# Attention in plain float32: scores and V product without split operands, the mask added in PSUM, one maximum per group

## The chip, the core and the metric

The kernel runs on one core of a Trainium2 chip. The metric is the device time of one execution in microseconds. The core has five engines that work through their own instruction queues and wait for each other by semaphores: TensorE (PE in the profile; its weight loads are PEld), VectorE (DVE), ScalarE (ACT), GpSimd (POOL, called the Pool here) and SyncE (SP), which starts transfers here.

## The reference, cut to what matters

Eight batches of 256 rows with 256 columns go through a cross attention with 16 heads and then through a mixture of eight experts. Both have a layer norm ahead and a residual. The attention is the part that changes:

```python
kv_c = kv @ W_kvc
q_c = q @ W_dq
q_nope = (q_c @ W_uq).reshape(b, lq, H, HD).transpose(0, 2, 1, 3)
q_rope = (q_c @ W_qr).reshape(b, lq, H, R).transpose(0, 2, 1, 3)
...
scores = (jnp.einsum('bhqd,bkhd->bhqk', q_nope, k_nope) + jnp.einsum('bhqr,bkr->bhqk', q_rope, k_rope)) * scale
k_ids = jnp.arange(lk)[None, None, :]
qs = seg_id[:, :, None]
good = (k_ids <= qs) & (k_ids >= qs - LOOKBACK)
scores = jnp.where(good[:, None, :, :], scores, NEG)
attn = jax.nn.softmax(scores, axis=-1)
out = jnp.einsum('bhqk,bkhd->bqhd', attn, v).reshape(b, lq, H * HD)
return out @ W_o
```

The feed forward part computes all eight experts (`relu(x @ expert_w + expert_b)`, 256 to 256 each) and averages the two with the highest gate logits. All data are float32. A row sees at most nine keys, and the segment ids are such that all of them lie in the first 128 keys; a second path for other ids exists in the kernel and isn't taken.

## The kernel before

Weights are folded beforehand: W_uk into W_uq, W_uv into W_o, so that a head works on vectors of 128 (64 latent, 64 rotary) against keys `kT` and on values `v` of 64. Rows are worked in 16 tiles of 128. A group is four heads of one tile (`HG = 4`), so there are 64 groups, four per tile and eight per batch.

The work is a software pipeline written out by hand in `slot(b, k)`, one such function for each engine, called by `walk`. Slot i works on several groups at once. In the order of TensorE's queue it holds: the query product of group i+1 (three products of float32r parts, 512 columns), the scores of group i, the four transposes of prob of group i-1, the product with W_o of group i-2, the gate product in one slot of four, the four transposes of q of group i+1, the transposes of x2n in one slot of four, the experts of group i-8 (a bf16 product of three rows that adds the bias, then six of 512 columns) and the V product of group i-1. In the slots 1 to 7 the latent product `latent` (L504) and transposes of the next batch's rows (`x_turn`, L489) stand in the place of the experts. Slots of batches 2 to 6 run in a loop of eight slots (`Fori`), the others are written out.

Products for which float32 accuracy is wanted are made of float32r parts: an operand is split into a rounded `hi` and the rest `lo`, and `mm3` adds hi by hi, hi by lo and lo by hi. For the scores both operands are split: ScalarE casts the transposed q to `qT_hi` (L1011), VectorE subtracts to `qT_lo` (L1235), and `kT_hl` holds both parts of the keys side by side, split once a batch by VectorE (L1251, L1253). Per head one product of qT_hi with both halves (256 columns, L883) and one of qT_lo with the first half (128 columns, L884) fill one of four 256-column strips in two PSUM banks. VectorE then adds the mask to the second half of the strips (`s2m`, L1192), and for each head one step (L1199) adds the halves, scales by -SCALE, writes the negated scores `nsc` to SBUF and their minimum to `nmax`. ScalarE computes four exponentials from `nsc` (L1023) with their sums, VectorE the reciprocals (L1272), and the Pool scales prob (L1114). After the transposes ScalarE casts to `pT_hi` (L1007) and VectorE subtracts to `pT_lo` (L1218). The V product (mm3, L550 to L552) uses `v_hi` and `v_lo`, which hold the 64 columns of v between two blocks of zeros, so that a slice of 128 weight columns puts the even heads on the lower and the odd ones on the upper half of the partitions: six products of 256 columns, all with 128 weight columns.

The Pool builds the mask of the next tile in three steps over slots g = 1 to 3 (L1100, L1104, L1109). VectorE's two rope products (L1176, L1177) and the Pool's join (L1062) stand between the query product and the transposes of q (L924). At the start `fold_o` (L446) folds W_uv into W_o by plain float32 products with 64 weight columns; their output goes to the lower and the upper 64 partitions in turn.

Of the kernel before, what the change touches and what calls it, by code (L numbers as in the profile page):

```python
# [53 lines left out]
def kernel_program(nc, x, ctx_t, itok, w_kvc, w_dq, w_uq_t, w_qr, w_uk_t, w_kr, w_uv_t, w_o,  # L54
                   gate_w, gate_b, expert_w, expert_b, rope, w_kvc_t, out):
    with ExitStack() as ctx:
# [20 lines left out]
        ident = sb("ident", [P, P])  # L77
        kidx = sb("kidx", [P, P])
# [13 lines left out]
        v_hi, v_lo = sb("v_hi", [P, 3, KVC], F32R), sb("v_lo", [P, 3, KVC], F32R)  # L92
# [94 lines left out]
        def _(act):  # L187
# [56 lines left out]
        def _(dve):  # L244
# [22 lines left out]
            dve.tensor_copy(kidx[:], kidx_i[:]).then_inc(S("kidx_done"), 1)  # L267

# [96 lines left out]
        def gb(name, shape, dt=F32):  # L365
# [21 lines left out]
        qT_hi = [sb(f"qT_hi{i}", [P, HG, P], F32R) for i in range(2)]  # L387
        qT_lo = [sb(f"qT_lo{i}", [P, HG, P], F32R) for i in range(2)]
        nsc = [sb(f"nsc{i}", [P, HG, P]) for i in range(2)]
# [4 lines left out]
        pT_hi = [sb(f"pT_hi{i}", [P, HG, P], F32R) for i in range(2)]  # L394
        pT_lo = [sb(f"pT_lo{i}", [P, HG, P], F32R) for i in range(2)]
        oT_hi = [sb(f"oT_hi{i}", [P, 2, P], F32R) for i in range(2)]
        oT_lo = [sb(f"oT_lo{i}", [P, 2, P], F32R) for i in range(2)]
        kT_hl = sb("kT_hl", [P, 2, P], F32R)
        s2m = sb("s2m", [P, HG, P])
        m_after, m_before, mask = sb("m_after", [P, P]), sb("m_before", [P, P]), sb("mask", [P, P])  # L400
# [3 lines left out]
        B_S = psum[:, 4 * 512:6 * 512].rearrange("p (h a n) -> p h a n", h=HG, a=2)  # L404
# [11 lines left out]
                 "nope_copied", "qT_hi_done", "exp_done", "pT_hi_done", "oT_hi_done", "xT_hi_done", "relu_done",  # L416
                 "rope_parts", "qT_lo_done", "score_max", "recip_done", "pT_lo_done", "oT_lo_done", "x2_done",
                 "ln_step", "x2n_done", "xT_lo_done", "gates_ready", "gate_step", "logit_part", "qc_split", "mask_step", "k_split",
                 "v_split", "v_hi_done", "x_normed", "x_turned", "x_columns", "latent_mm", "latent_sb", "wo_hi_done",
                 "wo_lo_done", "fold_o_mm", "we_hi_done", "we_lo_done", "k_hi_done", "qc_hi_done", "s2_masked", "waits_passed",  # L420
# [9 lines left out]
        def live(i, end):  # L430
            return not isinstance(i, int) or 0 <= i < end
# [427 lines left out]
        def _(pe):  # L859
            def slot(b, k):  # L860
# [28 lines left out]
                if live(i - 1, GROUPS):  # L889

                    at_least(pe, "prob_normed", i)
                    at_least(pe, "pT_hi_done", i - 1)
                    at_least(pe, "pT_lo_done", i - 1)
# [23 lines left out]
                if live(i + 1, GROUPS):  # L917
# [3 lines left out]
                    at_least(pe, "qT_hi_done", i + 1)  # L921
                    at_least(pe, "qT_lo_done", i + 1)
# [36 lines left out]
                if live(i - 1, GROUPS):  # L959

                    if (k - 1) % SLOTS == 0:
                        at_least(pe, "v_split", b + (k - 1) // SLOTS + 1)
# [385 lines left out]
```

## Time and profile before

| | us |
|---|---|
| median of 3 runs | 456.32 (456.17 to 457.66) |
| span of the profiled execution | 454.5 |

| engine | busy us | share of the span |
|---|---|---|
| TensorE, products | 422.4 | 93% |
| TensorE, weight loads | 355.9 | 78% |
| VectorE | 365.4 | 80% |
| ScalarE | 289.3 | 64% |
| Pool | 265.7 | 58% |

The profiled execution's own time is known by its span, from its first to its last instruction; the median of the runs is 1.8 us more. Busy time says that an engine had an instruction under way. TensorE's instructions overlap: the records of a product and of the next one cover each other, so the share of TensorE is not the share of its peak. What a block of products costs is read from the times at which it and the block behind it start. The share is also a mean over stages: the preparation up to some 26 us, the early slots to 87 us, the even stretch of 54 slots to 417 us, and the drain, in which experts alone are left.

### The profile page before, as it was taken

To read this page: it belongs to the slowest core of one execution; us is meant where nothing else is said; L and a number is where in the kernel's file an instruction comes from. 1 tells how busy PE (TensorE), PEld (TensorE's weight loads), DVE (VectorE), ACT (ScalarE), POOL (GpSimd) and SP (SyncE) were. 2 spreads that over 40 slices of the span, in tenths; PEclk is the share of its full clock that TensorE was granted. 3 is DMA by queue.
4 is the path that set the end of the run, shared out by engine and by line. 5 is a ranking of instruction groups with operands and counts; after the bars stand their busy time and mean duration, and the time that the engine had idled before them with its cause. 6 is when DMAs were issued, how large, how long until landed. Compare 5 with 4: busy or idle time off the path is not lost.

```text
span 454.5 us, 10511 instructions
## 1 busy us (share of the span) xinstructions
PE 422.4 (93%) x2702; PEld 355.9 (78%) x2702; DVE 365.4 (80%) x1369; ACT 289.3 (64%) x940; POOL 265.7 (58%) x365
## 2 busy tenths in 40 slices
PE   2966998899999999999999999999999999999995
PEld 2835887778888888878888888788888888788763
DVE  2659989897888888888889798988888888978541
ACT  1224766667676767677766767676776677667632
POOL 4033646647666747575765657575746575664545
PEclk9967999999999999999999999999999999999999
DMA  9990000000000000000000000000000000000000
GB/s 216 276 377 18 2 1 1 0 3 1 12 2 13 1 14 2 12 0 12 0 0 12 0 12 0 12 0 12 0 12 0 12 0 12 2 2 12 2 12 29
DMA packets 16530, 12.54 MB, mean 28 GB/s; under 512 B 7568, under 2 KB 16128, under 8 KB 16240
## 3 DMA queue, kind: packets, MB, share of 16 engines
q1 hardware_dynamic: 13488, 10.64, 7.9%
q10 hardware_dynamic: 2880, 1.43, 1.4%
q8 instruction: 14, 0.23, 0.2%
q14 instruction: 20, 0.16, 0.1%
q0 software_dynamic: 128, 0.09, 0.1%
HBM read 10.04 MB, written 2.10 MB: 27 GB/s over the span
## 4 chain that ended last, share of the span: by engine, by line
issue 39%; PE 25%; POOL 19%; DVE 7%; ACT 2%; POOLq 1%; DVEq 0%; ACTq 0%
POOL acc L1088 7%; PE psum L550 6%; PE psum L552 5%; PE psum L551 5%; POOL acc L1091 3%; PE psum L924 2%; PE psum L883 2%; PE psum L895 2%; POOL m_after L1100 2%; POOL m_before L1104 2%; POOL q_sb L1062 2%; ACT prob L1023 1%; DVE xn L477 1%; PE psum L954 1%; POOL rstd L1074 1%
## 5 line engine op out<-in xcount | busy, mean ns | idle before, releaser
L1114 POOL TENSOR_TENSOR prob<-prob,prec 128x512 f32<-128x512 f32 x64 | 68.6, 1071 | 91.6 <-DVE prec L1272 91.6
L1023 ACT ACTIVATE prob<-nsc,nmax 128x128 f32<-128x128 f32 x256 | 99.8, 395 | 3.7 <-DVE nmax L1199 3.7
L1062 POOL TENSOR_TENSOR q_sb<-rope_a,rope_b 128x256 f32<-128x256 f32 x64 | 47.0, 735 | 56.2 <-DVE rope_b L1177 56.2
L1199 DVE CUSTOM_DVE_ANT_0 nsc<-psum,s2m 128x128 f32<-128x128 f32 x256 | 59.1, 287 | 13.8 <-DVE s2m L1192 13.8
L1044 ACT ACTIVATE eout<-psum,gates 128x256 f32<-128x256 f32 x128 | 54.0, 477 | 19.0 <-DVE gates L1281 9.5
L1011 ACT CAST qT_hi<-psum 128x512 fp32r<-128x512 f32 x64 | 37.6, 587 | 43.7 <-PE psum L924 43.6
L883 PE MATMUL psum<-kT_hl,qT_hi 128*128 128x256 f32 x256 | 63.1, 324 | 0.0
L884 PE MATMUL psum<-kT_hl,qT_lo 128*128 128x128 f32 x256 | 57.4, 224 | 0.0
L550 PE MATMUL psum<-we_hi,xT_hi 128*128 128x512 f32 x128 | 57.2, 447 | 0.0
L884 PEld LDWEIGHTS psum<-kT_hl,qT_lo 128*128 128x128 f32 x256 | 49.6, 194 | 2.7
L883 PEld LDWEIGHTS psum<-kT_hl,qT_hi 128*128 128x128 f32 x256 | 48.9, 191 | 2.7
L552 PE MATMUL psum<-we_hi,xT_lo 128*128 128x512 f32 x128 | 50.5, 394 | 0.0
L551 PE MATMUL psum<-we_lo,xT_hi 128*128 128x512 f32 x128 | 50.3, 393 | 0.0
L1091 POOL TENSOR_TENSOR acc<-acc,eout 128x256 f32<-128x256 f32 x64 | 46.7, 729 | 5.0
L1023 ACT ACTIVATION_READ_ACCUMULATOR prob<-nsc,nmax 128x1 f32 x256 | 49.0, 191 | 0.0
L1192 DVE TENSOR_TENSOR s2m<-psum,mask 128x512 f32<-128x512 f32 x64 | 43.9, 686 | 3.9 <-PE psum L884 0.8
L999 ACT COPY q_sb<-psum 128x256 f32<-128x256 f32 x64 | 23.9, 373 | 36.3 <-DVE rope_b L1177 35.6
L924 PE MATMUL psum<-ident,q_sb 128*128 128x128 f32 x256 | 41.0, 284 | 5.6 <-POOL q_sb L1062 4.5
L1166 DVE TENSOR_TENSOR oT_lo<-psum,oT_hi 128x256 fp32r<-128x256 f32 x64 | 26.9, 420 | 21.3 <-ACT oT_hi L1029 21.2
L1218 DVE TENSOR_TENSOR pT_lo<-psum,pT_hi 128x512 fp32r<-128x512 f32 x64 | 43.9, 686 | 0.0
L1235 DVE TENSOR_TENSOR qT_lo<-psum,qT_hi 128x512 fp32r<-128x512 f32 x64 | 43.4, 677 | 0.3 <-ACT qT_hi L1011 0.3
L1029 ACT CAST oT_hi<-psum 128x256 fp32r<-128x256 f32 x64 | 23.8, 371 | 29.5 <-PE psum L552 29.4
(145 smaller groups left out, 1153.0 us busy)
## 6 DMA issues: line engine op xcount, KB each, us to landing
wo_raw<-in_w_o SPq DMA_DIRECT2D x2, 1024.0 KB, 10.6
we_raw<-in_expert_w SPq DMA_DIRECT2D x1, 2048.0 KB, 14.7
out<-acc SPq DMA_DIRECT2D x16, 128.0 KB, 1.7
x_all<-in_x SPq DMA_DIRECT2D x2, 640.0 KB, 7.8
ctxT<-in_ctx_t SPq DMA_DIRECT2D x2, 512.0 KB, 7.3
wuqT<-in_w_uq_t ACTq DMA_DIRECT2D x1, 768.0 KB, 13.1
wukT<-in_w_uk_t SPq DMA_DIRECT2D x1, 512.0 KB, 11.1
x_all<-in_x SPq DMA_DIRECT2D x1, 512.0 KB, 12.9
```

The lines of the kernel that those rows point to most:

```text
L550: pe.matmul(out_ap, l_hi, r_hi, start=start, stop=False)
L551: pe.matmul(out_ap, l_hi, r_lo, start=False, stop=False)
L552: return pe.matmul(out_ap, l_lo, r_hi, start=False, stop=stop)
L883: pe.matmul(B_S[:, h, :, :], qT_hi[r][:, h, :], kT_hl[:], start=True, stop=False)
L884: mm = pe.matmul(B_S[:, h, 0, :], qT_lo[r][:, h, :], kT_hl[:, 0, :], start=False, stop=True)
L924: mm = pe.transpose(B_QT[:, P * h:P * h + P], q_sb[1 - r][:, h, :], ident[:])
L1023: e = act.activation(prob[r][:, h, :], nsc[r][:, h, :], ACT.Exp, bias=nmax[r][:, h:h + 1], scale=-1.0, accum_out=psum_h[r][:, h:h + 1])
L1044: a = act.activation(eout[r][:, e, :], expert_bank(f)[:, O * e:O * e + O], ACT.Relu, scale=gates[j][:, 2 * kc + e:2 * kc + e + 1])
L1062: pool.tensor_tensor(q_sb[1 - r][:, :, KVC:P], rope_a[1 - r][:], rope_b[1 - r][:], ALU.add).then_inc(m["rope_joined"], 1)
L1091: pool.tensor_tensor(acc[j][:], acc[j][:], eout[1 - r][:, 1, :], ALU.add).then_inc(m["acc_step"], 1)
L1114: pool.tensor_tensor(p[:], p[:], prec[r][:, :].unsqueeze(2).to_broadcast([P, HG, P]), ALU.mult).then_inc(m["prob_normed"], 1)
L1199: e = dve.tensor_tensor_reduce(nsc[r][:, h, :], B_S[:, h, 0, :], s2m[:, h, :], -SCALE, BIG, ALU.add, ALU.min, nmax[r][:, h:h + 1])
```

## The change

The scores are one plain float32 product per head (`qT` as it comes out of the transposes, keys from `kT_all`), and the V product is two plain float32 products with 64 weight columns (`v_cur`), written to the lower and the upper half of the partitions. The casts to `hi` on ScalarE become copies of the same size; the subtractions `qT_lo`, `pT_lo`, the splits of k and v and the tiles for them are gone. `kT_all` is scaled by SCALE when it is copied in the preparation. The mask is held in bf16, in two buffers, and a product of a bf16 identity with the mask (512 columns, the mask repeated for four heads) starts each group's bank, to which the heads' scores are added. The scores of a group fill one bank, and two banks alternate. VectorE takes one maximum over the bank for all four heads, and ScalarE's exponentials read PSUM. Waits change with this: the scores wait for the exponentials of two groups before instead of the maximum of the last, and, in a tile's first group, for the mask.

```diff
@@ -210,8 +211,8 @@
-                act.copy(kT_all[:, 4 * i:4 * i + 4, :],
-                         bank[i].rearrange("p (b k) -> p b k", b=4)).then_inc(S("kT_sb"), 1)
+                act.mul(kT_all[:, 4 * i:4 * i + 4, :],
+                        bank[i].rearrange("p (b k) -> p b k", b=4), SCALE).then_inc(S("kT_sb"), 1)
...
@@ -224,9 +225,6 @@
-            pool.memset(v_hi[:].bitcast(F32), 0.0).then_inc(S("v_zero"), 1)
-            pool.memset(v_lo[:].bitcast(F32), 0.0).then_inc(S("v_zero"), 1)
...
@@ -265,6 +263,8 @@
+            dve.wait_ge(S("ident_done"), 1)
+            dve.tensor_copy(ident16[:], ident[:]).then_inc(S("ident16_done"), 1)
...
-        B_S = psum[:, 4 * 512:6 * 512].rearrange("p (h a n) -> p h a n", h=HG, a=2)
+        B_S = [bank[4 + i].rearrange("p (h n) -> p h n", h=HG) for i in range(2)]
...
@@ -874,14 +870,15 @@
-                    if k % SLOTS == 0:
-                        at_least(pe, "k_split", b + k // SLOTS + 1)
-                    at_least(pe, "qT_hi_done", i + 1)
-                    at_least(pe, "qT_lo_done", i + 1)
-                    at_least(pe, "score_max", i)
+                    at_least(pe, "qT_sb", i + 1)
+                    at_least(pe, "exp_done", i - 1)
+                    if g == 0:
+                        at_least(pe, "mask_step", 4 * (t + 1))
+                    keys = kT_all[:, bass.ds(b + k // SLOTS, 1), :].rearrange("p a n -> p (a n)")
+                    pe.matmul(B_S[r], ident16[:], mask[(k // GPT) % 2][:, :].unsqueeze(1).to_broadcast([P, HG, P]),
+                              start=True, stop=False)
                     for h in range(HG):
-                        pe.matmul(B_S[:, h, :, :], qT_hi[r][:, h, :], kT_hl[:], start=True, stop=False)
-                        mm = pe.matmul(B_S[:, h, 0, :], qT_lo[r][:, h, :], kT_hl[:, 0, :], start=False, stop=True)
+                        mm = pe.matmul(B_S[r][:, h, :], qT[r][:, h, :], keys, start=False, stop=(h == HG - 1))
...
@@ -969,14 +963,9 @@
                     q1 = 1 - r
-                    o = B_O[:, 0:D]
                     for odd in range(2):
-                        w = slice(KVC - KVC * odd, P + KVC - KVC * odd)
-                        vh = v_hi[:].rearrange("p a n -> p (a n)")[:, w]
-                        vl = v_lo[:].rearrange("p a n -> p (a n)")[:, w]
-
-                        mm = mm3(pe, o, vh, vl, pT_hi[q1][:, odd::2, :], pT_lo[q1][:, odd::2, :],
-                                 start=(odd == 0), stop=(odd == 1))
+                        mm = pe.matmul(B_O[KVC * odd:KVC * odd + KVC, 0:D], v_cur[:], pT[q1][:, odd::2, :],
+                                       start=True, stop=True)
...
@@ -1020,7 +1009,7 @@
-                        e = act.activation(prob[r][:, h, :], nsc[r][:, h, :], ACT.Exp, bias=nmax[r][:, h:h + 1], scale=-1.0,
+                        e = act.activation(prob[r][:, h, :], B_S[r][:, h, :], ACT.Exp, bias=nmax[r][:, h:h + 1],
...
@@ -1105,8 +1094,8 @@
-                    at_least(pool, "s2_masked", i + 1)
-                    pool.tensor_tensor(mask[:], m_before[:], m_after[:], ALU.add).then_inc(m["mask_step"], 1)
+                    at_least(pool, "s_done", i - 3)
+                    pool.tensor_tensor(mask[(k // GPT + 1) % 2][:], m_before[:], m_after[:], ALU.add).then_inc(m["mask_step"], 1)
...
@@ -1181,24 +1170,12 @@
-                    dve.tensor_copy(v_hi[:, 1:2, :], kv).then_inc(m["v_hi_done"], 1)
-                    dve.wait_ge(m["v_hi_done"], bv + 1)
-                    dve.tensor_tensor(v_lo[:, 1:2, :], kv, v_hi[:, 1:2, :].bitcast(F32), ALU.subtract).then_inc(m["v_split"], 1)
+                    dve.tensor_copy(v_cur[:], kv.rearrange("p a n -> p (a n)")).then_inc(m["v_ready"], 1)
                 if live(i, GROUPS):
 
                     at_least(dve, "s_done", i + 1)
-                    if g == 0:
-                        at_least(dve, "mask_step", 4 * (t + 1))
-                    dve.tensor_tensor(s2m[:], B_S[:, :, 1, :], mask[:, :].unsqueeze(1).to_broadcast([P, HG, P]),
-                                      ALU.add).then_inc(m["s2_masked"], 1)
-                if live(i, GROUPS):
-                    at_least(dve, "s2_masked", i + 1)
                     at_least(dve, "exp_done", i - 1)
-                    carry_wait()
-                    for h in range(HG):
-                        e = dve.tensor_tensor_reduce(nsc[r][:, h, :], B_S[:, h, 0, :], s2m[:, h, :], -SCALE, BIG,
-                                                     ALU.add, ALU.min, nmax[r][:, h:h + 1])
-                    e.then_inc(m["score_max"], 1)
+                    dve.tensor_reduce(nmax[r][:], B_S[r], AX.X, ALU.max, negate=True).then_inc(m["score_max"], 1)
...
@@ -1212,11 +1189,6 @@
-                if live(i - 1, GROUPS):
-                    at_least(dve, "pT_hi_done", i)
-                    at_least(dve, "pv_done", i - 2)
-                    dve.tensor_tensor(pT_lo[1 - r][:], B_PT[:, :].rearrange("p (h n) -> p h n", h=HG),
-                                      pT_hi[1 - r][:].bitcast(F32), ALU.subtract).then_inc(m["pT_lo_done"], 1)
...
@@ -1229,11 +1201,6 @@
-                if live(i + 1, GROUPS):
-                    at_least(dve, "qT_hi_done", i + 2)
-                    at_least(dve, "s_done", i)
-                    dve.tensor_tensor(qT_lo[1 - r][:], B_QT[:, :].rearrange("p (h n) -> p h n", h=HG), qT_hi[1 - r][:].bitcast(F32),
-                                      ALU.subtract).then_inc(m["qT_lo_done"], 1)
```

## Rows read from the trace of the kernel before

**Rows 1.** The page, part 1: busy us (share of the span) and instructions of TensorE and VectorE.

```profile
PE 422.4 (93%) x2702; PEld 355.9 (78%) x2702; DVE 365.4 (80%) x1369; ACT 289.3 (64%) x940; POOL 265.7 (58%) x365
```

**Rows 2.** Timeline of TensorE, one slot (start us, length us, engine, line, operation, tiles).

```profile
246.76 0.40 PE L550 MATMUL psum<-wq_hi,qc_hi 96*128 96x512 f32 x1
...
247.45 0.28 PE L883 MATMUL psum<-kT_hl,qT_hi 128*128 128x256 f32 x1
...
248.33 0.62 PE L895 MATMUL psum<-ident,prob 128*128 128x128 f32 x4
...
249.49 0.60 PE L924 MATMUL psum<-ident,q_sb 128*128 128x128 f32 x4
250.03 0.38 PE L954 MATMUL psum<-bias,ones 3*128 3x512 bf16 x1
...
251.60 0.39 PE L552 MATMUL psum<-we_hi,xT_lo 128*128 128x512 f32 x1
251.83 0.28 PE L550 MATMUL psum<-pT_hi,v_hi 128*128 128x256 f32 x1
...
252.54 0.40 PE L550 MATMUL psum<-wq_hi,qc_hi 96*128 96x512 f32 x1
```

**Rows 3.** Waits of weight loads, 87.4 to 417 us (waiter, releaser, total us, times, longest).

```profile
PEld psum L924 <- POOL q_sb L1062: 4.0, 14, 0.3
```

**Rows 4.** Busy time by stretch (length; PE, PEld, DVE, ACT, POOL; granted clock, DMA).

```profile
87.40:417.00 329.60, 325.94 (x2132) 278.48 (x2133) 283.93 (x1082) 230.75 (x767) 206.47 (x280) 1.00 0.02 6
...
48.87:87.32 38.45, 34.32 (x234) 29.37 (x233) 35.34 (x120) 26.62 (x89) 22.33 (x25) 1.00 0.01 1
```

**Rows 5.** Chain that ended last, in order of time, 20 to 90 us (start, length).

```profile
33.54 0.69 DVE qT_lo L1235
...
34.69 1.65 DVE st_all L155 x5
...
38.31 0.61 DVE s2m L1192
...
40.05 1.21 DVE wo_lo L456 x2
...
58.77 0.67 PE psum L924 x4
...
65.02 0.67 PE psum L924 x4
...
87.32 0.47 PE psum L550
```

**Rows 6.** Timeline of TensorE: plain float32 products, latent and in the preparation.

```profile
53.00 1.03 PE L504 MATMUL psum<-xnT,wdq 128*96 128x256 f32 x4
...
16.49 0.39 PE L333 MATMUL psum<-wcat,ctxT 128*128 128x128 f32 x2
```

**Rows 7.** Line L504 alone (length ns: shortest, median, longest; first and last start).

```profile
L504 PE MATMUL psum<-xnT,wdq x28: 379/379/379, 46.7 to 85.1; 128*96 128x256 f32 x28
```

**Rows 8.** Timeline of the weight loads in the slot of rows 2: the bias.

```profile
250.02 0.09 PEld L954 LDWEIGHTS psum<-bias,ones 3*128 3x128 bf16 x1 [0.17 <-issue]
```

**Rows 9.** Timeline of TensorE, 32.4 to 35 us: folding of W_o and its neighbours.

```profile
32.46 0.42 PE L924 MATMUL psum<-ident,q_sb 128*128 128x128 f32 x1
32.81 1.99 PE L446 MATMUL psum<-wo_raw,wuvT 128*64 128x256 f32 x16
34.73 0.50 PE L550 MATMUL psum<-wq_hi,qc_hi 96*128 96x512 f32 x1
```

**Rows 10.** Instructions by line and shape (count; busy us, mean ns; idle before).

```profile
L1192 DVE TENSOR_TENSOR s2m<-psum,mask 128x512 f32<-128x512 f32 x64 | 43.9, 686 | 3.9 <-PE psum L884 0.8
L1218 DVE TENSOR_TENSOR pT_lo<-psum,pT_hi 128x512 fp32r<-128x512 f32 x64 | 43.9, 686 | 0.0
...
L1261 DVE CAST qc_hi<-qc_all 96x128 fp32r x10 | 3.3, 335 | 0.0
...
L1261 DVE CAST qc_hi<-qc_all 96x128 fp32r<-96x128 f32 x6 | 1.6, 267 | 1.9 <-issue 1.9
```

More of the change, by code:

```diff
@@ L77, in kernel_program @@
         ident = sb("ident", [P, P])
+        ident16 = sb("ident16", [P, P], BF16)
         kidx = sb("kidx", [P, P])
@@ L89, in kernel_program @@
         flag = sb("flag", [1, 1], I32)
-        v_hi, v_lo = sb("v_hi", [P, 3, KVC], F32R), sb("v_lo", [P, 3, KVC], F32R)
+        v_cur = sb("v_cur", [P, KVC])
         block_sems = {}
@@ L386, in kernel_program @@
         rope_b = [sb(f"rope_b{i}", [P, HG, R]) for i in range(2)]
-        qT_hi = [sb(f"qT_hi{i}", [P, HG, P], F32R) for i in range(2)]
-        qT_lo = [sb(f"qT_lo{i}", [P, HG, P], F32R) for i in range(2)]
-        nsc = [sb(f"nsc{i}", [P, HG, P]) for i in range(2)]
+        qT = [sb(f"qT{i}", [P, HG, P]) for i in range(2)]
         nmax = [sb(f"nmax{i}", [P, HG]) for i in range(2)]
@@ L393, in kernel_program @@
         prec = [sb(f"prec{i}", [P, HG]) for i in range(2)]
-        pT_hi = [sb(f"pT_hi{i}", [P, HG, P], F32R) for i in range(2)]
-        pT_lo = [sb(f"pT_lo{i}", [P, HG, P], F32R) for i in range(2)]
+        pT = [sb(f"pT{i}", [P, HG, P]) for i in range(2)]
         oT_hi = [sb(f"oT_hi{i}", [P, 2, P], F32R) for i in range(2)]
         oT_lo = [sb(f"oT_lo{i}", [P, 2, P], F32R) for i in range(2)]
-        kT_hl = sb("kT_hl", [P, 2, P], F32R)
-        s2m = sb("s2m", [P, HG, P])
-        m_after, m_before, mask = sb("m_after", [P, P]), sb("m_before", [P, P]), sb("mask", [P, P])
+        m_after, m_before = sb("m_after", [P, P]), sb("m_before", [P, P])
+        mask = [sb(f"mask{i}", [P, P], BF16) for i in range(2)]
         B_Q, B_E, B_QT, B_PT, _, _, B_Y, B_X = bank
-        B_S = psum[:, 4 * 512:6 * 512].rearrange("p (h a n) -> p h a n", h=HG, a=2)
+        B_S = [bank[4 + i].rearrange("p (h n) -> p h n", h=HG) for i in range(2)]
         B_O = B_X
@@ L415, in kernel_program @@
         names = general_names + ["q_done", "qT_done", "s_done", "pT_done", "pv_done", "y_done", "xT_done", "gate_done", "e_done",
[L416 to L420, printed above, removed]
+                 "nope_copied", "qT_sb", "exp_done", "pT_sb", "oT_hi_done", "xT_hi_done", "relu_done",
+                 "rope_parts", "score_max", "recip_done", "oT_lo_done", "x2_done",
+                 "ln_step", "x2n_done", "xT_lo_done", "gates_ready", "gate_step", "logit_part", "qc_split", "mask_step",
+                 "v_ready", "x_normed", "x_turned", "x_columns", "latent_mm", "latent_sb", "wo_hi_done",
+                 "wo_lo_done", "fold_o_mm", "we_hi_done", "we_lo_done", "qc_hi_done", "waits_passed",
                  "rope_joined", "prob_normed", "rstd2_done", "acc_step", "out_stored0", "out_stored1"]
@@ L961, in slot @@
                     if (k - 1) % SLOTS == 0:
[L962 to L964 removed]
+                        at_least(pe, "v_ready", b + (k - 1) // SLOTS + 1)
+                    at_least(pe, "pT_sb", i)
                     at_least(pe, "oT_hi_done", i - 1)
@@ L1006, in slot @@
                     at_least(act, "pv_done", i - 2)
-                    act.copy(pT_hi[1 - r][:], B_PT[:, :].rearrange("p (h n) -> p h n", h=HG)).then_inc(m["pT_hi_done"], 1)
+                    act.copy(pT[1 - r][:], B_PT[:, :].rearrange("p (h n) -> p h n", h=HG)).then_inc(m["pT_sb"], 1)
                 if live(i + 1, GROUPS):
@@ L1010, in slot @@
                     at_least(act, "s_done", i)
-                    act.copy(qT_hi[1 - r][:], B_QT[:, :].rearrange("p (h n) -> p h n", h=HG)).then_inc(m["qT_hi_done"], 1)
+                    act.copy(qT[1 - r][:], B_QT[:, :].rearrange("p (h n) -> p h n", h=HG)).then_inc(m["qT_sb"], 1)
                 if g == 3 and live(t - 1, TILES):
@@ L1245, in slot @@
                     top_two("gate_step", t - 2, [3, 4])
-                bk = b + (k + 1) // SLOTS
-                if (k + 1) % SLOTS == 0 and live(bk, B):
-                    at_least(dve, "s_done", SLOTS * bk)
-                    kk = kT_all[:, bass.ds(bk, 1), :].rearrange("p a n -> p (a n)")
-                    dve.tensor_copy(kT_hl[:, 0, :], kk).then_inc(m["k_hi_done"], 1)
-                    dve.wait_ge(m["k_hi_done"], bk + 1)
-                    dve.tensor_tensor(kT_hl[:, 1, :], kk, kT_hl[:, 0, :].bitcast(F32), ALU.subtract).then_inc(m["k_split"], 1)
                 tq = TPB * b + k // GPT + 1
```

8 lines of the change are left out of this document (2 added, 6 removed).

## The prediction

> **What bounds the kernel now.** I read the busy shares first, then TensorE's order of work in one slot of the steady stretch, then who waits for whom. TensorE is busy 93% of the span, VectorE 80% [rows 1]. A busy TensorE proves little, since its instructions overlap: the pitch from start to start has to tell. In the slot that starts at 246.76 every block follows the last one without a gap [rows 2]: three query products to 247.45 (0.69 us), scores to 248.33 (0.88), transposes of prob and the output product to 249.49 (1.16), transposes of q to 250.03 (0.54), experts to 251.83 (1.80), V product to 252.54 (0.71): 5.78 in all. From 87.4 us on the clock is granted in full [rows 4], and the only data for which TensorE's loads wait are 14 late q_sb, 4.0 us in all [rows 3]; none waits for prob, pT or the scores. There the order of TensorE sets the time, and all that VectorE saves is worth those waits. Before 87.32 it is otherwise: six slots take 38.45 us [rows 4], and the chain runs from the transposes of q over exponentials, VectorE's xn, rope and the Pool's join back to the transposes, from 58.77 to 65.02, 6.25 long [rows 5]. VectorE's large subtractions aren't in that loop.
>
> **TensorE's blocks after the change.**
>
> Scores. Each of the four heads had one product of 256 columns and one of 128, with 0.22 a head [rows 2]. By the pace of the 512-column query products (0.23 each) their 384 columns would stream in 0.17: it is the two weight loads that fill the head's time. A plain float32 product appears as two records with a weight load each: the latent product is two products in the code and four records in the trace, which at 256 columns and full clock lie (1.03 - 0.38) / 3 = 0.22 apart, twice their columns' time [rows 6, 7]. With 128 columns the same form stands in the preparation: two records in 0.39 [rows 6], and a record alone lasts about 0.38 - 0.11 = 0.27 (128 columns less), so they are 0.11 to 0.12 apart. Eight of them make 0.90, so +0.02; ends 0 and +0.08. Streaming costs more, but the loads cost as much already. The Trainium skill (FP8 and Floating Point Precision, TensorE Precision Notes) says that true FP32 takes four passes through the array. The latent product's rows agree, but by columns alone the scores would go from 384 to 512 a head and cost a third more (+0.29), and by the row of the preparation they don't.
>
> Mask. One more product of 512 columns, in bf16 with 128 x 128 weights, goes ahead of the scores. Nearest row: a 512-column product among its like, 0.23 [rows 2]. The only bf16 product in the trace, the experts' bias with three rows, costs more. Its load starts at 250.02, 0.07 before the transposes end (249.49 + 0.60), and stood 0.17 idle [rows 2, 8]; the experts' block of 1.80 is six products at 0.23 (1.39) and 0.41 more. So the bias costs up to 0.58. Ends: 0.21 (the columns alone) and 0.58. But the plain float32 product with 64 weight columns shows the same hold of a load until the product ahead has nearly ended (below), while the products with 96 rows or columns show none: few rows or columns go with the hold, not bf16. The mask's uses all 128 by 128, so I take 0.23.
>
> V product. Six f32r products at 0.12 (0.71) become two plain float32 ones with 64 weight columns, four records. The folding of W_o has the same form: 128 x 64 weights, 256 columns, the two halves of the partitions in turn. Its 16 records at full clock take 1.99, so they are (1.99 - 0.38) / 15 = 0.107 apart, half of the latent product's pitch: two run side by side. They start at 32.81, 0.07 before the product ahead ends (32.46 + 0.42), and the query product behind starts at 34.73 and lasts 0.50 instead of 0.40 [rows 9, 2]. From 32.81 to 34.73 are 1.92 us; eight pairs at 0.215 are 1.72, so the edges cost 0.20 beyond them, and two pairs would take 0.43 + 0.20 = 0.63. In the slot the experts' last product ends at 251.60 + 0.39 = 251.99, so V's first load starts at 251.92 and the query product at 252.55: where it starts now. Only the query block grows by the exposed load, 0.10. So +0.11 for both. Ends: no hold at either side, 0.43 for 0.71 (-0.28); no records side by side, two more pitches (+0.54). I take +0.11, since [rows 9] show its very form. The rule that stands behind them is in the Trainium skill (TensorEngine Tiling, Key Properties): changing the tiling mode drains TensorE. It speaks against this edit, which leaves 128 weight columns for 64 and goes back once a slot; the rows agree.
>
> A slot grows by 0.02 + 0.23 + 0.11 = 0.36 us. The groups 8 to 63 have their scores and V products in the TensorE-bound part: 56 x 0.36 = +20.2 us.
>
> **What is given back.** VectorE loses s2m (0.69 us), four score steps (some 0.86), pT_lo (0.69) and qT_lo (as long), and gains one maximum over 128 x 512 in PSUM, which I price like s2m's one pass, 0.7 [rows 10]: 2.2 us less a slot. In the steady stretch this is worth the waits for q_sb, which stand behind rope and the Pool's join. The transposes of q now come 0.11 + 0.23 + 0.02 later in the slot, which covers a wait of 0.28: -4.0 [rows 3]. In the early slots the added 0.36 fits (5.78 + 0.36 is under 6.25), and six turns of 6.25 are 37.5 instead of 38.45: -1.0. At the start qT_lo and the split of kT (33.54 to 34.69) and s2m with the score steps (38.31 to 40.05) lie on the chain [rows 5]: 1.15 + 1.74 - 0.7 = 2.2 off; the first slots run in part at half clock and pay some 0.6 more for mask and scores: -1.6.
>
> At nothing I cost: the small copy to ident16 and the two fills that go (VectorE and the Pool wait for loads and TensorE then); the exponentials from PSUM instead of SBUF, as no wait of TensorE names prob, with 0 to 0.28 a slot if that cover went and the waits came back 56-fold; the bank pair, which replaces a wait for the maximum by one for exponentials two groups back. Keys and v_cur's source are addressed by a register: VectorE's qc_hi takes 335 ns so, and 267 with a fixed address [rows 10], so 0 to 0.07 for each of four products, 0.28 a slot. I take none, since TensorE's instructions queue ahead of their data.
>
> Sum: 454.5 + 20.2 - 4.0 - 1.0 - 1.6 = 468.1 us of span. The median of the runs stands 1.8 above the profiled span, so 469.9.
>
> **The rivals.**
> 1. As forecast, slower, 470: chance 0.71. Its own bounds: -0.1 a slot if a part of the hold is missed (-5.6), or +0.03 for the scores (+1.7) and q_sb waits that stay (+4.0): 464 to 476.
> 2. The mask's bf16 product holds the loads at both sides as the bias does, 0.35 more a slot, or the register addresses cost 0.28: 56 times, +16 to +20, 486 to 490. For: every bf16 product in the trace has the hold. Against: so have the float32 ones with few columns. Chance 0.15.
> 3. The V product goes without the hold: its loads slip in behind the experts' last product and the query product follows at once. A slot then changes by -0.28 + 0.23 + 0.02 = -0.03, and 456.3 - 1.7 - 6.6 = 448.0: faster. It decides once the V product with its edges takes under 0.58 (then 56 slots add just the 6.6 given back). For: the side-by-side pitch of 0.107 is real. Against: the hold is there in [rows 8, 9]. Chance 0.09, and 0.04 for an outcome near that point.
> 4. VectorE's 2.2 us a slot show in the steady stretch after all; then TensorE must have waited for it, and [rows 3] leave 4.0 us for that. Chance 0.01, faster.
>
> A measurement of this kernel can tell about 0.3% from no change. From these cases: faster 0.10, same 0.04, slower 0.86. The range leaves out the faster cases and the outer half of the second, and reaches down for a hold missed at one side: 462 to 487.
>
> **What would show it.** A mask product 0.23 before the first score; eight score records 0.11 to 0.12 apart; V's four records in 0.6, the first load 0.07 before the experts' end, and a query product of 0.50; slots without extras 6.14 long; no wait for q_sb after 90 us; VectorE near 50% of the span. The prediction is wrong if the mask's load waits for the end of the query product, if V's load overlaps the experts, or if the slots are longer than these blocks add up to.

## The result and the profile after

| | before | after |
|---|---|---|
| median of 6 runs, us | 456.25 (455.7 to 457.66) | 459.33 (458.34 to 460.19) |
| span of the profiled execution, us | 454.5 | 457.6 |

The ratio of the medians is 1.0061, with a 95% interval of 1.0044 to 1.0077: slower by 3.1 us, where 469.9 was forecast with a range of 462 to 487. The sign was right, and the size was missed by 10.6 us, below the range.

The busy shares of the page after, to be held against [rows 1]:

```profile
PE 431.5 (94%) x2638; PEld 317.1 (69%) x2638; DVE 250.6 (55%) x706; ACT 280.8 (61%) x940; POOL 264.9 (58%) x363
```

VectorE is busy for 115 us less, and TensorE for 9 us more. The time moved by 3, so the two don't simply exchange.

TensorE's timeline after, one slot without extras (start us, length us, engine, line, operation, tiles), to be held against [rows 2]:

```profile
264.28 0.50 PE L546 MATMUL psum<-wq_hi,qc_hi 96*128 96x512 f32 x1
...
265.09 0.39 PE L878 MATMUL psum<-mask,ident 128*128 128x512 bf16 x1
265.31 1.05 PE L881 MATMUL psum<-kT_all,qT 128*128 x8
266.21 0.60 PE L891 MATMUL psum<-ident,prob 128*128 128x128 f32 x4
266.56 0.37 PE L546 MATMUL psum<-wo_hi,oT_hi 128*128 128x256 f32 x1
...
267.36 0.60 PE L919 MATMUL psum<-ident,q_sb 128*128 128x128 f32 x4
267.89 0.38 PE L949 MATMUL psum<-bias,ones 3*128 3x512 bf16 x1
268.21 0.50 PE L546 MATMUL psum<-we_hi,xT_hi 128*128 128x512 f32 x1
...
269.80 0.65 PE L967 MATMUL psum<-pT,v_cur 128*64 128x256 f32 x4
270.38 0.50 PE L546 MATMUL psum<-wq_hi,qc_hi 96*128 96x512 f32 x1
```

From start to start: query product 0.81 us (0.69 in [rows 2]), mask 0.22, scores 0.90 (0.88), transposes and output product 1.15 (1.16), transposes of q 0.53 (0.54), experts 1.91 (1.80), V product 0.58 (0.71). That is 6.10 for 5.78. Records have an error of 0.01 each; over many slots the mask is 0.23, the scores 0.89, and the slots g = 0, 2 and 3, which wait in neither kernel, go from 6.22 to 6.51, from 5.79 to 6.09 and from 6.01 to 6.32: +0.30. The letter g is the place of a slot's group in its tile. A slot g = 1 goes from 6.03 to 6.10, or from 6.6 to 6.7 in seven cases, to 6.09.

The 54 slots from the start of slot 8 to that of slot 62, before and then after (stretch and length; PE, PEld, DVE, ACT, POOL; granted clock, DMA), and the waits of weight loads in this stretch after:

```profile
87.32:417.26 329.94, 326.28 (x2134) 278.82 (x2135) 284.26 (x1084) 230.83 (x767) 206.53 (x280) 1.00 0.02 6
82.67:420.46 337.79, 337.79 (x2083) 248.23 (x2081) 189.30 (x526) 224.55 (x770) 206.27 (x281) 1.00 0.02 6
```

```profile
PEld psum L546 <- issue: 33.4, 109, 0.4
PEld psum L967 <- issue: 19.1, 53, 0.4
PEld psum L878 <- issue: 14.7, 54, 0.3
PEld psum L949 <- issue: 9.1, 54, 0.2
PEld psum L967 <- DVE eq_in L1143: 0.4, 1, 0.4
```

Before, TensorE had no record under way for 329.94 - 326.28 = 3.66 us of it; after, it is busy in all of the 337.79. The late q_sb of [rows 3] are gone. So these 54 slots are 7.85 us longer, what lies ahead of them is 4.65 shorter (slot 8 starts at 82.67, not 87.32 as in [rows 5]), and the drain is the same to 0.1 us: +3.1.

But 54 x 0.30 is 16.2, not 7.85. Of the missing 8.35 us the waits of [rows 3] are 4.0. The rest is in the trace of before, where I had not seen it. The waits of TensorE's products before, 87.4 to 417 us (waiter, what ended the wait, total us, times, longest), then TensorE and VectorE around one of the seven:

```profile
PE psum L550 <- issue: 2.6, 7, 0.4
```

```profile
147.47 0.39 PE L552 MATMUL psum<-we_hi,xT_lo 128*128 128x512 f32 x1
148.22 0.36 PE L550 MATMUL psum<-pT_hi,v_hi 128*128 128x256 f32 x1 [0.37 <-issue]
...
149.01 0.40 PE L550 MATMUL psum<-wq_hi,qc_hi 96*128 96x512 f32 x1
```

```profile
144.56 0.76 DVE L1186 TENSOR_TENSOR v_lo<-kcat,v_hi 128x64 fp32r<-128x64 f32 x1
145.25 0.68 DVE L1192 TENSOR_TENSOR s2m<-psum,mask 128x512 f32<-128x512 f32 x1
...
147.34 0.68 DVE L1218 TENSOR_TENSOR pT_lo<-psum,pT_hi 128x512 fp32r<-128x512 f32 x1
```

In [rows 2] the V product starts 0.23 after the last expert product (251.60, 251.83); here 0.75 after it. It starts 0.20 after pT_lo ended (147.34 + 0.68 = 148.02), and its block is 0.79 long instead of 0.71. pT_lo is late because v_lo (0.76, once a batch) stands ahead of s2m, the score steps, x and pT_lo on VectorE. The seven come 48.8 to 48.9 us apart, once a batch: 7 x 0.60 = 4.2 us. 16.2 - 4.0 - 4.2 = 8.0, against 7.85 measured. After the change there is no pT_lo, and TensorE doesn't wait for one.

### The profile page after: what moved, and what is told of

Same layout as the page of the kernel before. It is cut to its first block, busy times and chain, and to the rows that moved or that the text cites. A ratio compares the mean times of both kernels' runs of the same rounds, so it can differ in the third digit from the quotient of the medians.

```text
span 457.6 us, 9458 instructions
## 1 busy us (share of the span) xinstructions
PE 431.5 (94%) x2638; PEld 317.1 (69%) x2638; DVE 250.6 (55%) x706; ACT 280.8 (61%) x940; POOL 264.9 (58%) x363
## 4 chain that ended last, share of the span: by engine, by line
PE 81%; POOL 4%; issue 3%; DVE 3%; ACT 2%; DVEq 0%; POOLq 0%; ACTq 0%
PE psum L546 17%; PE psum L548 12%; PE psum L547 12%; PE psum L881 11%; PE psum L967 7%; PE psum L919 6%; PE psum L891 5%; PE psum L949 4%; PE psum L878 3%; ACT prob L1012 1%; POOL q_sb L1051 1%; POOL acc L1077 1%; POOL acc L1080 1%; PE psum L442 1%; DVE xn L473 1%
## 5 line engine op out<-in xcount | busy, mean ns | idle before, releaser
L1012 ACT ACTIVATE prob<-psum,nmax 128x128 f32<-128x128 f32 x256 | 91.2, 377 | 0.0
L881 PEld LDWEIGHTS psum<-kT_all,qT 128*128 128x128 f32 x512 | 68.0, 193 | 1.6
L881 PE MATMUL psum<-kT_all,qT 128*128 (+1 forms) x512 | 67.5, 275 | 0.0
L1000 ACT COPY qT<-psum 128x512 f32<-128x512 f32 x64 | 37.5, 586 | 42.7 <-PE psum L919 42.7
L1012 ACT ACTIVATION_READ_ACCUMULATOR prob<-psum,nmax 128x1 f32 x256 | 55.2, 216 | 0.0
L1178 DVE TENSOR_REDUCE nmax<-psum 128x4 f32<-128x512 f32 x64 | 44.2, 690 | 16.0 <-PE psum L881 15.5
L996 ACT COPY pT<-psum 128x512 f32<-128x512 f32 x64 | 37.7, 588 | 19.2 <-PE psum L891 18.9
L546 PE MATMUL psum<-wo_hi,oT_hi 128*128 128x256 f32 x128 | 41.7, 326 | 1.0 <-DVE oT_lo L1155 1.0
L967 PE MATMUL psum<-pT,v_cur 128*64 128x256 f32 x256 | 41.7, 404 | 0.4 <-DVE xT_lo L1202 0.4
L891 PE MATMUL psum<-ident,prob 128*128 128x128 f32 x256 | 38.6, 273 | 1.3 <-POOL prob L1103 1.3
## 6 DMA issues: line engine op xcount, KB each, us to landing
wo_raw<-in_w_o SPq DMA_DIRECT2D x2, 1024.0 KB, 10.5
```

Source lines behind the costliest of these rows:

```text
L546: pe.matmul(out_ap, l_hi, r_hi, start=start, stop=False)
L881: mm = pe.matmul(B_S[r][:, h, :], qT[r][:, h, :], keys, start=False, stop=(h == HG - 1))
L891: mm = pe.transpose(B_PT[:, P * h:P * h + P], prob[1 - r][:, h, :], ident[:])
L967: mm = pe.matmul(B_O[KVC * odd:KVC * odd + KVC, 0:D], v_cur[:], pT[q1][:, odd::2, :], start=True, stop=True)
L1012: e = act.activation(prob[r][:, h, :], B_S[r][:, h, :], ACT.Exp, bias=nmax[r][:, h:h + 1], accum_out=psum_h[r][:, h:h + 1])
```

## The experiments

The theory: TensorE's order of work sets the time, an edit is worth its blocks, and the kernel before had two kinds of waits in the steady stretch (q_sb, pT_lo), which a longer slot covers. The rival: VectorE's load itself costs there, so that its relief is what was given back. Each expectation says what its own A and B stand for. All ratios are to the kernel before, with 95% intervals.

**The wait for pT_lo by itself.** The kernel before without v_lo:

```diff
-                    dve.tensor_copy(v_hi[:, 1:2, :], kv).then_inc(m["v_hi_done"], 1)
-                    dve.wait_ge(m["v_hi_done"], bv + 1)
-                    dve.tensor_tensor(v_lo[:, 1:2, :], kv, v_hi[:, 1:2, :].bitcast(F32), ALU.subtract).then_inc(m["v_split"], 1)
+                    dve.tensor_copy(v_hi[:, 1:2, :], kv).then_inc(m["v_split"], 1)
```

> The kernel before, with one thing left out: the low part of v is not computed (it stays zero, so the V product is computed from the high part of v alone). This takes one VectorE subtraction of 0.76 us out of the first V slot of each batch. Theory A: the seven slots of the kernel before in which the V product starts 0.5 us late (labelled issue) wait for VectorE's pT_lo, which stands behind this subtraction; then these slots fall from 6.7 to about 6.1 and the time falls by 7 x 0.5 to 0.6, to 452 to 453. Rival B: they are the edge of the loop (branch and instruction fetch); then nothing moves, 456.

Measured: 451.69 us, 0.9906 (0.9892 to 0.992), span 450.2, 4.3 shorter. The slot of the same place, TensorE:

```profile
146.69 0.40 PE L552 MATMUL psum<-we_hi,xT_lo 128*128 128x512 f32 x1
146.93 0.28 PE L550 MATMUL psum<-pT_hi,v_hi 128*128 128x256 f32 x1
```

0.24 from the last expert product to the V product. Of the waits for weight loads, those for q_sb stay at 4.1 us in 14. One VectorE instruction of 0.76 us, eight times in the kernel, had cost 4.3 us.

**VectorE's load put back.** The kernel after, with the subtractions and a masking step on VectorE again; their results are not used, but TensorE waits for them at the old places:

```diff
+                    dve.tensor_tensor(v_lo[:], kv, v_hi[:].bitcast(F32), ALU.subtract).then_inc(m["v_ready"], 1)
...
+                    dve.tensor_tensor(s2m[:], B_S[r], ident[:, :].unsqueeze(1).to_broadcast([P, HG, P]), ALU.add).then_inc(m["s2_masked"], 1)
...
+                    dve.tensor_tensor(pT_lo[:], B_PT[:, :].rearrange("p (h n) -> p h n", h=HG),
+                                      pT[1 - r][:], ALU.subtract).then_inc(m["pT_lo_done"], 1)
...
+                    dve.tensor_tensor(qT_lo[:], B_QT[:, :].rearrange("p (h n) -> p h n", h=HG),
+                                      qT[1 - r][:], ALU.subtract).then_inc(m["qT_lo_done"], 1)
```

> The changed kernel with VectorE's removed work put back as idle work into tiles that nobody uses (a pass over the scores, pT_lo, qT_lo, the split of v), and TensorE waiting for it as before. The result is the same as that of the changed kernel. Theory A: VectorE's relief gave back what the forecast missed, at the start and in the early slots (some 4 us) and in the late V products; then the time rises by 3 to 6 us, to 462 to 465, and the start of the eighth slot moves from 82.7 back to some 86 us. It isn't the whole 10 us, as the longer slots now cover a part of the old waits. Rival B: VectorE's relief is worth nothing and TensorE's order alone sets the time: 459.

Measured: 461.08 us, 1.0122 (1.0104 to 1.0139), between the two. The 54 slots with VectorE's load back:

```profile
83.38:421.10 337.72, 337.72 (x2080) 248.19 (x2080) 275.91 (x702) 224.87 (x768) 206.53 (x281) 1.00 0.02 6
```

337.72 us, the same as without the load (337.79), though VectorE is busy for 275.9 us instead of 189.3. So what was put back costs nothing in the steady stretch once TensorE's slot is 0.3 longer. It is not all of the old load: this kernel has no split of k and one maximum instead of four score steps, and that matters. VectorE and TensorE around the V product of such a slot here:

```profile
142.14 0.65 DVE L1183 TENSOR_TENSOR v_lo<-kcat,v_hi 128x64 fp32r<-128x64 f32 x1
...
144.37 0.68 DVE L1207 TENSOR_TENSOR pT_lo<-psum,pT 128x512 fp32r<-128x512 f32 x1
```

```profile
145.39 0.65 PE L973 MATMUL psum<-pT,v_cur 128*64 128x256 f32 x4
```

The V product starts 0.34 after pT_lo's end (145.05), where the late ones of before started 0.20 after it: a margin of 0.14. From the start of v_lo to the end of pT_lo are 2.91 us, before 3.46 (144.56 to 148.02). With the old score steps these V products would still be some 0.3 to 0.4 us late, of 0.6 (0.55 less the margin, and less 0.1 for a copy of v that only this kernel has ahead of v_lo); that is an estimate from these rows, and no run shows it. By it the longer slot alone covers the smaller part of the seven late V products, and VectorE's relief the larger.

Ahead of that stretch the load does cost: slot 0 takes 6.11 us instead of 4.60 (1.5 of that was won before it, where the folding was done sooner), and slots 2 to 7 take 37.20 instead of 36.36 and are uneven again (5.67 to 6.71). Slot 8 starts 0.7 us later (83.38, 82.67), and that is all that the two profiled executions differ by (458.3, 457.6); the medians differ by 1.75, and the rest is in no trace.

**One half of the change at a time.** First the kernel before with the new V product alone:

```diff
-                        mm = mm3(pe, o, vh, vl, pT_hi[q1][:, odd::2, :], pT_lo[q1][:, odd::2, :],
-                                 start=(odd == 0), stop=(odd == 1))
+                        mm = pe.matmul(B_O[KVC * odd:KVC * odd + KVC, 0:D], v_cur[:], pT[q1][:, odd::2, :],
+                                       start=True, stop=True)
```

> The kernel before with the new V product alone (plain float32, 64 weight columns, no pT_lo, no split of v). By the blocks of the changed kernel the V product with its edges costs 0.58 + 0.10 + 0.11 against 0.71, +0.08 a slot, +4.5 us; the late V products (4.2 us) go with pT_lo, and of the q_sb waits a part. Theory A: 454 to 456. Rival B (the seven late V products are the loop's edge): 458 to 460.

Measured: 453.34 us, 0.9942 (0.9929 to 0.9955), 0.7 below theory A. This half is faster. Its blocks (query 0.80, experts 1.90, V 0.58) cost 0.07 a slot, +3.9 on 56; no product waits for pT_lo any more, -4.2; the waits for q_sb fall from 4.0 to 2.5 us; slot 8 starts 0.8 earlier. That is -2.6, for -3.0 of span measured.

Then the rest of the change with the old V product (the same lines the other way round):

> The changed kernel with the V product of the kernel before (three f32r parts, 128 weight columns, pT_lo and the split of v on VectorE). Blocks: +0.23 a slot for the mask, +12.9 us; given back are the q_sb waits (4.3), the late V products (VectorE is 1.5 us lighter a slot, 4.2) and some 3 at the start. Theory A: 457 to 459. Rival B (VectorE's relief worth only the q_sb waits): 464 to 466.

Measured: 455.85 us, 0.9999 (0.999 to 1.0009): no difference from before, and 1.2 below theory A, which had some 3 us for the start. Mask and scores cost 54 x 0.24 = 13.0 us; back come 4.2, 4.0, and 5.2 from the early slots (slot 8 starts at 82.13). The gain ahead of slot 8 belongs to this half, not to the V product: six slots of some 6.11 us instead of the uneven 5.79 to 7.15 of before. v_lo and pT_lo are both in this kernel, TensorE's slot is only 0.24 longer, and still pT_lo ends 0.9 us or more ahead of the V product in the slots that were late before. There VectorE's lighter work around the scores covers the wait, with 0.7 us to spare.

**The mask's product left out.** The softmax runs over all keys, so the output is another:

```diff
-                    pe.matmul(B_S[r], ident16[:], mask[(k // GPT) % 2][:, :].unsqueeze(1).to_broadcast([P, HG, P]),
-                              start=True, stop=False)
```

> The changed kernel without the mask product: no mask is added, so the softmax runs over all keys. Theory A (the product costs TensorE its 0.23 in each slot, and the chain transposes of q, exponentials, reciprocal, gates, rope, join, back to the transposes, 6.11 long in the kernel before, binds again once a tile): 56 x 0.23 = -12.9 and 14 x 0.1 to 0.2 back, 448 to 450. Rival B (bf16 product hidden in part, or a wait takes its place): over 453.

Measured: 447.48 us, 0.9802 (0.9784 to 0.9819), 11.9 less than after, 0.5 below theory A. 56 x 0.23 is 12.9; the 54 slots give 10.8 of it (one slot g = 3 in eight slots stays at 6.25 in five batches, 0.16 over its like), and 0.9 comes ahead of them. Query product 0.80 and scores 0.89 are what they were with the mask between them: no edge at either side. The second rival's bf16 hold isn't there. No load waits for q_sb either, though the transposes of q stand only 0.11 later in the slot than before, where the new V product alone, with the same 0.11, left 2.5 us of these waits. So the lighter score steps cover them too, without the mask's 0.23.

**The mask added by VectorE instead.** It has the time: the score step adds it, with a float32 mask.

```diff
-                    dve.tensor_reduce(nmax[r][:], B_S[r], AX.X, ALU.max, negate=True).then_inc(m["score_max"], 1)
+                    for h in range(HG):
+                        e = dve.tensor_tensor_reduce(nsc[r][:, h, :], B_S[r][:, h, :], mask[(k // GPT) % 2][:], -1.0, BIG,
+                                                     ALU.add, ALU.min, nmax[r][:, h:h + 1])
+                    e.then_inc(m["score_max"], 1)
```

> The changed kernel with the mask added by VectorE: per head one step adds the float32 mask to the scores and takes the extreme, as the kernel before did with s2m, and the exponentials read SBUF. No mask product. Theory A: TensorE's 0.23 a slot go as in the kernel without a mask, VectorE's step costs 0.86 instead of 0.69 and is covered: 448 to 450, equal to the run without a mask within 1. Rival B (VectorE's step is on the path again): over 453.

Measured: 450.43 us, 0.9865 (0.9847 to 0.9882), 8.9 less than after and 3.0 more than without any mask, so above theory A, which had at most 1 for that. VectorE's four steps lengthen the loop of the early slots from 6.12 to 6.26, and the loads wait 2.2 us for q_sb again.

**Few rows or bf16?** The experts' bias product holds the loads around it. It has three rows and is bf16. Here its operands have 128 partitions, 125 of the bias's filled with zeros; type and columns stay:

```diff
-        bias3 = sb("bias3", [3, NE * O], BF16)
-        ones3 = sb("ones3", [3, P], BF16)
+        bias3 = sb("bias3", [P, NE * O], BF16)
+        ones3 = sb("ones3", [P, P], BF16)
...
+            pool.memset(bias3[:], 0.0).then_inc(S("bias_zero"), 1)
```

> The changed kernel with the experts' bias held on 128 partitions instead of 3, zeros in the others, and the ones too: the same bf16 product with 128 rows, the result is the same. Theory A (few rows, as few columns, make the loads wait until the product ahead is done, on both sides): the bias falls to 0.23, the transposes ahead of it to 0.37 from 0.53, some 0.3 a slot, -17 to -20 us in all less 2 to 4 for the 6.11 chain: 441 to 446. Rival B (bf16 next to float32r makes the loads wait): 459, nothing moves.

Measured: 444.5 us, 0.9732 (0.9714 to 0.9749). TensorE and then its weight loads, the same block:

```profile
265.43 0.60 PE L920 MATMUL psum<-ident,q_sb 128*128 128x128 f32 x4
265.87 0.38 PE L950 MATMUL psum<-bias,ones 128*128 128x512 bf16 x1
265.89 0.58 PE L547 MATMUL psum<-we_hi,xT_hi 128*128 128x512 f32 x1
266.31 0.39 PE L548 MATMUL psum<-we_lo,xT_hi 128*128 128x512 f32 x1
...
267.56 0.65 PE L968 MATMUL psum<-pT,v_cur 128*64 128x256 f32 x4
```

```profile
265.76 0.10 PEld L950 LDWEIGHTS psum<-bias,ones 128*128 128x128 bf16 x1
265.87 0.19 PEld L547 LDWEIGHTS psum<-we_hi,xT_hi 128*128 128x128 f32 x1
```

Both loads have lost their idle time of 0.17 and 0.23. The transposes of q give way after 0.44 instead of 0.53, the experts take 1.69 instead of 1.91. A slot without extras falls from 6.09 to 5.80, and 14.8 us go. The hold comes with few rows, not with bf16. The Trainium skill states for another tiling mode (TensorEngine Tiling, Key Properties): "Mode switching requires drain". The trace agrees if a product of three rows counts as such a switch, which neither that section nor the trace says; here one of them costs 0.29 us.

**The V product with 128 weight columns.** The same plain float32 operands, v between zeros as before, both halves summed in one tile:

```diff
-                        mm = pe.matmul(B_O[KVC * odd:KVC * odd + KVC, 0:D], v_cur[:], pT[q1][:, odd::2, :],
-                                       start=True, stop=True)
+                        w = slice(KVC - KVC * odd, P + KVC - KVC * odd)
+                        mm = pe.matmul(B_O[:, 0:D], v_cur[:].rearrange("p a n -> p (a n)")[:, w], pT[q1][:, odd::2, :],
+                                       start=(odd == 0), stop=(odd == 1))
```

> The changed kernel with the V product's weights 128 columns wide (v between zeros, as the kernel before, but plain float32). Four records of 256 columns can't lie side by side then. Theory A (64 weight columns give pairs, and make loads wait at both edges): the block goes from 0.58 to 4 x 0.216 = 0.86, and the edges, 0.10 in the experts' block and 0.11 in the query product, go: +0.07 a slot, 463. Rival B (the edges belong to plain float32, not to the columns): 0.28 a slot, 473 to 475.

Measured: 464.77 us, 1.0179 (1.0161 to 1.0197), 5.4 more than after. TensorE around this V product:

```profile
271.47 0.40 PE L549 MATMUL psum<-we_hi,xT_lo 128*128 128x512 f32 x1
271.70 1.03 PE L969 MATMUL psum<-pT,v_cur 128*128 128x256 f32 x4
272.38 0.58 PE L547 MATMUL psum<-wq_hi,qc_hi 96*128 96x512 f32 x1
272.80 0.39 PE L548 MATMUL psum<-wq_lo,qc_hi 96*128 96x512 f32 x1
```

The edge ahead is gone (271.70 is 0.23 behind the last expert product). The four records are spread over 0.68 and the first query product's pitch of 0.42, 0.19 over the usual 0.23: 0.87 in all, four times 0.22. With 64 columns the block takes 0.07 to 0.08 more than the old 0.71 in all, 0.78: 0.43 for two pairs side by side and 0.35 at the edges. With 128 columns it takes 0.87 and has no edge. So the edges go with 64 columns (the one ahead by its start, the one behind by this count), and even so 64 columns are the cheaper form, by 0.09 a slot. The old six float32r products at 0.71 beat both.

**The padded bias in the kernel before**, by the same lines as above, with nothing else changed.

> The kernel before, with nothing changed but the bias on 128 partitions. Theory A, that the hold of TensorE's loads ahead of and behind the three-row product is a cost of its own in both kernels: slots fall by some 0.25 to 0.3 us, 440 to 444 us, unless VectorE is late, which its waits would show (q_sb and pT_lo). Theory B, that VectorE stands close behind TensorE in this kernel (80% busy): much of the gain turns into waits for q_sb and pT_lo, 446 to 453 us.

Measured: 446.02 us, 0.9775 (0.9754 to 0.9795), the lower end of theory B. The slots without extras fall by 0.30, 16.2 us on 54. The 54 slots fall from 329.9 to 321.2 us, so 8.7 arrive; 1.1 more comes from the drain. The waits for weight loads between 80 and 400 us, and one V product:

```profile
PEld psum L925 <- POOL q_sb L1063: 7.6, 13, 0.6
```

```profile
145.85 0.39 PE L553 MATMUL psum<-we_hi,xT_lo 128*128 128x512 f32 x1
146.90 0.36 PE L551 MATMUL psum<-pT_hi,v_hi 128*128 128x256 f32 x1 [0.66 <-issue]
```

In the same stretch before, q_sb was late by 3.8 us in 13 (3.8 more now, and 4.2 more over all 14), and the late V products cost 0.9 instead of 0.6 each (1.05 behind the last expert product instead of 0.75), 2.1 us more on seven: 16.2 - 4.2 - 2.1 = 9.9. The other 1.2 us is open; some of the slots g = 3 and 0 are 0.07 us longer than their like. TensorE's shorter slot uncovers what the longer one of the change had covered.

**The two gains together.** The kernel after with the lines of the padded bias and those of the mask on VectorE:

> The kernel after the change, with the bias on 128 partitions (125 of them zeros) and with the mask added by VectorE in its score step instead of by a product. Each edit alone gave 444.5 us and 450.4 us, against 459.3 us: 14.8 and 8.9 less. Theory A, that TensorE's order of work still sets the time: both gains add, 434 to 438 us, slots without extras near 5.6 us. Theory B, that at such slots the loop over rope, the Pool's join and the transposes takes over (6.12 us a slot in the early slots): 440 to 450 us, with waits of the transposes of q for q_sb in most slots.

Measured: 436.63 us, 0.9572 (0.9556 to 0.9588). The two gains add, as in theory A (459.33 - 14.8 - 8.9 = 435.6); slots without extras take 5.56 us. Theory B shows in one slot of four: g = 1 takes 6.05, with late q_sb (6.8 us in 14 waits of weight loads).

Then the same with the six float32r products and the splits of before for V:

> The same with the V product of before (six float32r products with 128 weight columns, their splits on VectorE). Theory A, that TensorE's order sets the time: the old V product was worth 3.5 us alone, so 431 to 435 us. Theory B, that VectorE, which gets v_lo and pT_lo back (0.69 us a slot) beside the score steps, is now late with them or with rope: not faster than the kernel with the new V product, 436 to 446 us.

Measured: 434.52 us, 0.9525 (0.9509 to 0.9541), the best of all, 21.7 us under the kernel before. One slot of TensorE without extras (the bias product ahead of the first expert product has left no record in this slot), then the waits of TensorE's weight loads between 80 and 400 us:

```profile
117.99 0.40 PE L552 MATMUL psum<-wq_hi,qc_hi 96*128 96x512 f32 x1
...
118.68 1.05 PE L883 MATMUL psum<-kT_all,qT 128*128 128x128 f32 x8
...
121.19 0.58 PE L552 MATMUL psum<-we_hi,xT_hi 128*128 128x512 f32 x1
...
123.48 0.40 PE L552 MATMUL psum<-wq_hi,qc_hi 96*128 96x512 f32 x1
```

```profile
PEld psum L922 <- POOL q_sb L1060: 7.7, 14, 0.6
PEld psum L552 <- issue: 2.9, 13, 0.8
```

5.49 for a slot that took 5.79 before and 6.09 after. What is left in the way is q_sb in one slot of four: the loop over rope and the Pool's join begins to count.

## Why the prediction was wrong

The forecast span was 468.1, the span is 457.6: 10.5 us too much, in four terms. The step that failed is the sentence that all that VectorE saves in the steady stretch is worth the waits for q_sb, 4.0 us.

- **The late V products, 4.2 us: the step that failed.** The prediction said of TensorE that none of its loads waits for pT. That is so, but the wait is that of a product. I had read the waits of the weight loads only, and took "issue" for a wait on nothing. The seven waits stand among those of the products, with "issue" as their end. Their slots are 6.6 to 6.7 us long where slots of the same kind take 6.03 to 6.10; I had read one slot, one of those without a wait, and multiplied. The fourth rival (VectorE shows in the steady stretch after all) was held to 4.0 us for the same reason. It held in part, with a chance of 0.01. The experiment without v_lo showed these 4.2 us. With VectorE's load put back (but not its four score steps) nothing more is lost there: 337.72 us.
- **The blocks, 0.30 a slot instead of 0.36: 3.4 us on 56.** The mask was right (0.23 forecast and measured, and by the product left out). The scores came to +0.01, for 0.02, and the transposes of prob gave 0.01. The edges of the V product were right (experts 1.81 to 1.90, query product 0.69 to 0.80); its own block is 0.58, and 0.63 was forecast, since I left the folding's whole 0.20 of edge in it. So V with its edges costs +0.07, for 0.11.
- **Start and early slots: 4.65 us given back instead of 2.6: 2.1 us.** Slot 0 went from 7.40 to 4.60 and slots 2 to 7 from 38.45 to 36.36 us (6.12 a turn, not 6.25, and the last one, without the join's wait, 5.76). The half with the scores gives all of it. That VectorE's subtractions aren't in the loop was right for one turn, but the slots of before are uneven (5.79 to 7.15), and one typical turn did not price them. With VectorE's load put back they are uneven again and 0.84 of these 2.09 us return, 1.5 of the 2.8 of slot 0; the rest the runs don't separate. The 0.6 us for a clock at half in the first slots was not needed either: the granted clock was 0.84 in slot 0 and 0.67 in slot 1 before, behind a slot 0 in which TensorE was busy for 3.2 of 7.4 us, and it is 1.00 in both after. Slot 1 is no shorter for it (6.74, 6.77).
- **The drain, 0.7 us.** Groups 62 and 63 were counted like the others (56 groups); their slots have room, and the drain didn't grow.

What held: the -4.0 us for q_sb, though its reason, that the transposes of q come later in the slot, is one of two. The new V product alone moves them by 0.11 and takes 1.5 us of the waits, as that reason says; the kernel without the mask product moves them by no more and has none of them, by the lighter score steps. Also the hold of the loads at few rows or columns; the exponentials from PSUM, the bank pair and the register addresses at nothing. The exponentials and their sums on the page after, beside 395 and 191 ns before:

```profile
L1012 ACT ACTIVATE prob<-psum,nmax 128x128 f32<-128x128 f32 x256 | 91.2, 377 | 0.0
...
L1012 ACT ACTIVATION_READ_ACCUMULATOR prob<-psum,nmax 128x1 f32 x256 | 55.2, 216 | 0.0
```

The list of what would show it: the mask at 0.23, eight score records 0.11 apart, a query product of 0.50, no wait for q_sb after 90 us and VectorE near half (55%) came as named; slots of 6.14 were 6.09.

By columns, the wide V product is 0.87 us for two products of 256 columns, 0.44 each, and a head's scores of 128 columns are 0.22; four times the columns at the query product's pace (0.23 for 512) would be 0.46 and 0.23. That agrees with the four passes that the Trainium skill states for true float32 (FP8 and Floating Point Precision, TensorE Precision Notes). The scores didn't grow by a third all the same, since 384 columns of float32r had taken 0.22 too, in two products whose weight loads start 0.11 to 0.12 apart: a rule on the new form says nothing of what bounded the old one.

Of the rivals, the second is ruled out (no bf16 hold, by two runs, and four score products by register address at +0.01, not +0.28), and the third too (V with its edges takes 0.78, and 0.58 was its point of decision). That waits of before would pay for half of the added blocks no rival had. The sign came out right with little to spare: of the 16.2 us of blocks 3.1 were left.

## What to carry to other kernels

Before you price the relief of a side engine, list the lengths of all slots, not one, and read the products' waits as well as the loads'; a slot longer than its like points to a wait, whatever its label says. A gain on the bounding engine is paid out only as far as the next engine stands behind it, and a cost is taken only as far as no wait goes with it: 0.30 us a slot cost 7.85 instead of 16.2 us where it was added and VectorE relieved, and gave 8.7 instead of 16.2 where it was taken from the kernel before. Look at the odd small products: a bias product of three rows among full ones cost nearly five times what the whole change did.

## What was unexpected of the hardware

- A product of three rows among products of 128 costs 0.29 us beyond its own 0.23: 0.10 on the block ahead (its load waits) and 0.2 behind. Padded with zeros to 128 partitions, it costs 0.23 and no more. Over the kernel that is 14.8 us.
- Plain float32 with two times 64 weight columns runs its records in pairs (0.43 for four of 256 columns, by the pace of the folding), but pays 0.35 us on going there and back, from and to 128 columns: 0.78, for 0.87 with 128 columns and 0.71 with six float32r products.
- A bf16 product of full size between float32r and plain float32 ones costs its 0.23 us and nothing at its edges.
- A single VectorE instruction of 0.76 us once a batch reached TensorE as 0.6 us, with 2.7 us of other VectorE work between them (144.56 to 148.02 in all).
